# Moving the first projections one row tile ahead, with earlier weights and a quarter of the norms on ScalarE, in a sandwich transformer layer

## What is computed

```python
x = L0_attn_x                                   # (4, 4096, 1024), float32
x = x + layernorm(attn(layernorm(x)))           # 16 heads of 64, causal, ALiBi slopes
x = x + layernorm(ffn(layernorm(x)))            # 1024 -> 4096 -> 1024

# attn
q, k, v = heads(x @ Wq), heads(x @ Wk), heads(x @ Wv)
scores = einsum('bhqd,bhkd->bhqk', q, k) - slopes * dist
attn = softmax(where(causal, -inf, scores) / 8)
return einsum('bhqk,bhkd->bhqd', attn, v) @ Wo + bo
# ffn: x @ w1 + b1, rounded to 1/256, piecewise-linear GELU, @ w2 + b2, rounded
```

## Time and profile before

| | us |
|---|---|
| median of three runs | 1239.48 (1239.38 to 1240.03) |
| the profiled execution's own time | 1238.13 |
| its span, slowest core (6) | 1236.6 |
| spans of the eight cores | 1233.8 to 1236.6 |
| PE, ScalarE, VectorE, GpSimd busy | 1156.5, 984.7, 747.2, 178.7 |

### The profile page before, as it was taken

How to read it: one execution, slowest core, us unless ns; L and a number is a source line. 1 busy time by engine, 2 the same in 40 slices (tenths; PEclk the granted TensorE clock), 3 DMA queues, 4 the chain that set the end, 5 groups by cost and what they waited for, 6 DMA issues and landing times.

```text
span 1236.6 us, 27106 instructions; the slowest of 8 cores (1233.8 to 1236.6 us)
## 1 busy us (share of the span) xinstructions
PE 1156.5 (94%) x11298; PEld 641.0 (52%) x11298; DVE 747.2 (60%) x1607; ACT 984.7 (80%) x1219; POOL 178.7 (14%) x357
## 2 busy tenths in 40 slices
PE   3889989999999999999996999879999999999997
PEld 2566656656566565666654444433444444444443
DVE  7876443332434334343431689996888888888843
ACT  3449999999999999999999478887777777777720
POOL 4520010010100000000010344340111111111110
PEclk9999999999999999999999999999999999999999
DMA  9942543343533312111129664447333333443211
GB/s 260 276 149 55 102 71 58 58 86 61 92 57 70 65 32 52 27 32 27 33 50 171 225 199 155 147 127 161 110 109 112 110 111 112 128 128 111 77 68 69
DMA packets 62870, 128.00 MB, mean 104 GB/s; under 512 B 9238, under 2 KB 26134, under 8 KB 62108
## 3 DMA queue, kind: packets, MB, share of 16 engines
q1 hardware_dynamic: 53900, 101.10, 27.3%
q0 software_dynamic: 8848, 25.17, 13.0%
HBM read 117.84 MB, written 25.17 MB: 116 GB/s over the span
## 4 chain that ended last, share of the span: by engine, by line
PE 74%; DVE 12%; ACT 8%; DMA 3%; POOL 1%; issue 1%; SPq 0%; DVEq 0%; POOLq 0%; ACTq 0%
PE pW L898 18%; PE pF L825 14%; PE pjb L310 12%; PE S L403 9%; PE acc L456 9%; PE pjb L342 8%; ACT P L419 6%; DMA xst<-x_full 2%; DVE x L701 2%; PE pja L310 1%; DVE bst L229 1%; DVE bst L230 1%; DVE g L869 1%; DVE g L863 1%; DMA W<-wqkv 1%
## 5 line engine op out<-in xcount | busy, mean ns | idle before, releaser
L419 ACT ACTIVATE P<-S,biasT 128x1024 bf16<-128x1024 f32 (+1 forms) x576 | 563.0, 1083 | 21.2 <-PE S L403 19.5
L825 PE MATMUL pF<-xl2T,w1s 128*128 128x512 bf16 x1024 | 260.1, 383 | 11.2 <-ACT cu L840 11.2
L898 PE MATMUL pW<-w2s,hq 128*128 128x512 bf16 x1024 | 253.2, 380 | 3.0 <-ACT pW L923 3.0
L456 PEld LDWEIGHTS acc<-V,P 128*128 128x128 bf16 x4352 | 162.6, 97 | 53.0 <-DVE ctx L474 10.9
L403 PE MATMUL S<-Q,K 64*128 64x512 bf16 (+3 forms) x1280 | 174.9, 350 | 14.7 <-ACT P L419 12.8
L456 PE MATMUL acc<-V,P 128*128 128x66 bf16 x4352 | 180.0, 193 | 3.7 <-DVE ctx L474 2.0
L310 PE MATMUL pjb<-xlT,W 128*128 128x512 bf16 x648 | 167.1, 382 | 2.1 <-DVE kst L320 0.8
L825 PEld LDWEIGHTS pF<-xl2T,w1s 128*128 128x128 bf16 x1024 | 100.0, 99 | 132.3 <-ACT cu L840 13.2
L898 PEld LDWEIGHTS pW<-w2s,hq 128*128 128x128 bf16 x1024 | 100.2, 98 | 124.4 <-issue 4.0
L320 DVE CAST kst<-pjb 128x512 bf16<-128x512 f32 x81 | 56.0, 691 | 132.6 <-PE pjb L310 128.8
L840 ACT ACTIVATE cu<-pF,b1s 128x512 int32<-128x512 f32 x128 | 87.7, 685 | 58.7 <-PE pF L825 58.7
(11 more groups left out here) (80 smaller groups left out, 1079.8 us busy)
## 6 DMA issues: line engine op xcount, KB each, us to landing
w1s<-w1bf SPq DMA_DIRECT2D x128, 256.0 KB, 3.1
xst<-x_full SPq DMA_DIRECT2D x32, 512.0 KB, 10.1
K<-kst SPq DMA_DIRECT2D x128, 64.0 KB, 2.0
Q<-kst SPq DMA_DIRECT2D x128, 64.0 KB, 2.3
w1bf<-w POOLq DMA_DIRECT2D x32, 256.0 KB, 3.8
w2s<-w POOLq DMA_DIRECT2D x8, 1024.0 KB, 21.1
x<-x_full SPq DMA_DIRECT2D x16, 512.0 KB, 4.4
x2scr<-x SPq DMA_DIRECT2D x16, 512.0 KB, 3.0
```

The source lines that it names most:

```text
L419: t = put("scalar", lambda io: io.activation(out=P3[:, :, c0:512], in_=S[s][:].rearrange("p (o c) -> p o c", o=2)[:, :, c0:512], func=AF.E ...
L456: io.matmul(acc[:, q * 66:(q + 1) * 66], P[p][:, at:at + 128], zv[:, o, j, hh, :], start=st, stop=sp, skip_group_check=True),
L825: t = put("tensor", lambda io, c=c: io.matmul(pF[b][:], w1s[n % 4][:, c * 128:(c + 1) * 128], xl2T3[g][:, c, :], start=(c == 0), stop=(c = ...
L898: t = put("tensor", lambda io, ft=ft, hf=hf: io.matmul(pO[b][:, hf * 512:(hf + 1) * 512], slot_of(g, ft, tl), w2s[:, ft * 1024 + hf * 512: ...
```

## The change

Three edits. Every fourth tile (t % 4 == 3) is normed by ScalarE as an activation with a scale and a bias; for it `stats2` is asked for `nm`, minus the mean times `rs`, two GpSimd operations more. The weights of head pair 0 are requested in the iteration of tile 0 in place of tile 2; those of head pair 1 stay at tile 10. Pieces are put from the iteration of tile 8 on in place of tile 9, and a block is open one iteration sooner.

```diff
@@ -259,12 +259,17 @@
 
         def ln_a(t, t_x):
             k, tk = stats((xst[t % NX][:, 0:512], xst[t % NX][:, 512:1024]), [t_x])
-            return k, stats2(k, tk)
+            return k, stats2(k, tk, neg=t % 4 == 3)
 
         def ln_b(t, k, t_r):
-            tn = put("vector", lambda io: io.tensor_scalar(
-                out=xl[t % 4][:], in0=xst[t % NX][:], scalar1=mv[k][:, 0:1], scalar2=rs[k][:, 0:1],
-                op0=ALU.subtract, op1=ALU.mult), after=[t_r, xlfree[t % 4]], inc=True)
+            if t % 4 == 3:
+                tn = put("scalar", lambda io: io.activation(
+                    out=xl[t % 4][:], in_=xst[t % NX][:], func=AF.Identity, bias=nm[k][:],
+                    scale=rs[k][:, 0:1]), after=[t_r, xlfree[t % 4]], inc=True)
+            else:
+                tn = put("vector", lambda io: io.tensor_scalar(
+                    out=xl[t % 4][:], in0=xst[t % NX][:], scalar1=mv[k][:, 0:1], scalar2=rs[k][:, 0:1],
+                    op0=ALU.subtract, op1=ALU.mult), after=[t_r, xlfree[t % 4]], inc=True)
             xfree[t % NX] = tn
             slot_free[k] = [tn]
             tm = None
@@ -501,11 +506,11 @@
                 ln_b(*pend)
             if t + NX - 1 < 32:
                 t_load[t + NX - 1] = ln_load(t + NX - 1)
-            if t in (2, 10):
+            if t in (0, 10):
                 t_w[t // 10] = load_w(t // 10)
             pend = (t, k, t_r)
-            if t > 8:
-                pieces(4, (t - 1) // 8)
+            if t > 7:
+                pieces(4, t // 8)
         ln_b(*pend)
         if gen:
             for _ in gen:
```

## The result

The changed kernel takes 1244.37 us (median), the kernel before 1239.48; the ratio is 1.0036, 95% interval 1.0026 to 1.0046. The forecast was 1243.8. Some executions of every kernel here, three of nine of the changed one, are disturbed and some per cent longer, and no ratio uses them. The profiled execution took 1244.25 us with a span of 1242.7, against 1238.13 and 1236.6. That is 6.1 more, as the profiled execution before lies 1.35 under its median and this one at it; the medians differ by 4.9.

The account below looks back on a forecast made before the run. PE was taken to bound the kernel, with attention PE's own length; 0.3 + 2.17 - 1.0 + 4.9 - 0.2 + 0.1 - 2.0 = +4.3 us gave 1243.8 against the median 1239.48, range 1240.0 to 1247.2.

Parts of the forecast that it names:

- The norms on ScalarE: First stage: norms queue behind copy and kst eviction; tiles 15, 19, 27, 31 cost 4.9 us, tile 23 gains 0.2.
- Rival B: First stage: ScalarE's norms find it free, the 4.9 falls away, V intervals shrink; -1.6 us, or 1235 to 1238; chance 0.10.
- The head start: Projections from tile 8: late tile 7 uses up the tile gained; first projection at 29.7 to 30, an estimate.
- The landing: Head pair 1's weights in the first stage: land 0.3 us later, bounds -1.8 and +1.5; PE still waits some 2 us.
- the 44 that the prediction named as a sign of being wrong: First stage: the prediction is wrong if head pair 1's weights land before 44 us.
- Rival A: First stage: norms hurt as forecast, but pair 1's weights land 1.8 us early, no clock drop; +1.5, 1241.0; chance 0.18.
- the terms 0.3 + 2.17 - 1.0: Around pair 1's weights: landing 0.3 us later, one tile interval more behind it 2.17, low clock avoided 1.0.
- the 1.23 of tile 15: First stage, before tile 15's transposes: PE idles 1.23 us for the ScalarE norm, 3.40 against 2.17.
- costed at nothing as cover: First stage, tile 11: its ScalarE norm's delay hides under PE's stall for head pair 1's weights, so zero cost.
- The low clock: PE after the stall for pair 1's weights: a 2 us wait keeps 2.4 GHz; credit 1.0 of 1.67 us.
- the terms of the first stage: Up to the first score: 0.3 + 2.17 - 1.0 + 4.9 - 0.2 + 0.1 us, all terms but attention's.
- Attention: Attention stage, PE's own length: the V unit moved out gains 2.0 us, bounds 1.0 and 2.4.

Follow-up runs that it names:

- e1: Kernel before with only every fourth norm put on ScalarE; weights of head pair 0 at tile 2, pieces from tile 9 as before: ratio 1.0025, +3.1 us.
- e3: Changed kernel with only the ScalarE norm moved ahead in its queue, right behind its own tile's statistics: ratio 1.0001 against the kernel before.
- e2: Kernel before with weights of head pair 0 at tile 0 and pieces from tile 8, all norms on VectorE: ratio 1.0013, +1.6 us.
- e4: Kernel before with only the weights of head pair 0 asked for at tile 0: ratio 0.9985, -1.9 us.
- e8: Kernel before with one V unit moved from attention to the end of the first stage: no ratio on record, profiled execution 1240.82 us.
- e9: e4 with the norms of tiles 22, 23, 24, 29, 30 on ScalarE, put ahead in its queue: ratio 0.9956 against the kernel before, -5.5 us.

## Why the prediction was right, and where it was not

**The norms on ScalarE.** The step that decided. 3.40 us from T(t-1) to T(t) was forecast and 3.34 measured, at the four tiles named, and 2.9 at tile 23 (70.89 to 73.75, 2.86). From T(15) to T(31) core 6 took 42.48 us, 3.23 more than before; three such intervals less tile 23's gain were forecast at 3.5. e1 shows the cost by itself, e3 that it is the place in the queue. Rival B fell with it: even with the norms out of PE's way (e3) the time is that of the kernel before and not under it.

**The head start.** That tile 7 would use it up was right in kind: landing near 24 was forecast, its statistics start at 24.68. It was too small in size, as the first projection came at 31.48 and not near 30; tile 10's statistics are 0.9 late and not 0.3. The forecast's chain left out that the norm of tile 7, too, stands behind a copy: its statistics were complete at 28.23, the copy of tile 6 began at 28.02, and the norm at 28.93. PE was then to come to head pair 1's weights at about 44.5 and to wait 2 us; it came at 45.5 and didn't wait.

**The landing.** This step failed. The weights were to land near 46.6. On core 6 they landed 9.1 us behind the first request at 33.22, at 42.3, where the earlier trace rows has 14.0; on the eight cores at 42.1 to 46.0, against 44.9 to 46.8 before. Six of them are under the 44 that the prediction named as a sign of being wrong. Rival A had the earlier landing right, but not its time (1241.0): PE came too late to use it. Why they land sooner stays open. Tile 16's place in the queue is not enough: e2 has the same order of requests and 43.2 to 49.6, and e4, where tile 16 keeps its place, has them 1.1 sooner as well.

So the terms 0.3 + 2.17 - 1.0 are right in their sum and wrong as a path, and that is luck. No tile interval followed a landing; PE went on at its own pace. On the mean of the cores T(15) came 2.8 us later (50.3 to 53.1), where these terms and the 1.23 of tile 15 make 2.7. It is made up otherwise (an estimate from the rows). The first projection is 0.8 later, one tile interval more lies behind it (2.2), and the norms add 1.2 at tile 15 and 1.1 at tile 11. The stall of 2.3 is gone, and so is the low clock, 0.6 (1.67 on three of eight cores). About 0.4 is left over. Tile 11, costed at nothing as cover, counts in full once there is no stall to hide it.

**The low clock.** As forecast it is gone, but not because PE waited 2 us in place of 3: it did not wait for these weights at all. The credit of 1.0 was for the slowest core. The latest first score is 98.66 (core 5), against 93.28 before (core 4), +5.4, where the terms of the first stage add to +6.3. The mean core has +6.1.

**Attention.** This step failed. The moved V unit was to give 2.0 us, bounds 1.0 and 2.4. Attention is 0.6 shorter in the changed kernel, 0.9 from e4 to e2 and 0.5 in e8; as it is 0.4 shorter in e1 without such a unit, these are no finer than that. The reading of the earlier trace rows was at fault: 3.6 us of waiting for ScalarE in 547 was taken for "PE alone binds". The windows of core 6 before (columns as in the earlier trace rows) show both engines nearly full, PE busy for 98% and ScalarE for 96% of the stretch:

```profile
93.00:640.00 547.00, 537.69 (x7672) 336.78 (x7672) 214.41 (x576) 525.92 (x538) 28.46 (x63) 1.00 0.30 56
```

Work taken from one turned in large part into a wait for the other (PE's 3.6 became 4.6). The total came out within 0.6 by luck as well: this miss (1.4 too much gain) stands against the 0.2 to 0.9 by which the first stage was overstated, and against medians that lie closer together than the profiles.

**The edits apart.** The forecast costed the earlier weights at nothing but the landing's 0.3. By themselves they gain 1.9 us (e4). In its profile PE arrives later at a wait that it had anyway, the weights land a little sooner, and no clock is lost. In the whole change the stall and the low clock go in the same way.

## What to carry to other kernels

An instruction moved to an engine with idle time takes the place in that engine's queue that the program gives it: before pricing its duration, name what stands ahead of it there and whether that in turn waits for the engine you want to relieve. The same 1.24 us norm cost 1.2 us a tile behind such a copy and eviction, 0.3 ahead of them, and gained about 0.7 at tiles where the other engine's queue was the hold-up. A cost that is written off as hidden under a stall comes back when the same change removes the stall, as at tile 11. And where two engines are both over 95% busy, neither's waits alone price a unit of work: measure by moving one unit, as the answer here was a quarter to a half of its duration one way and more than half of it the other.

## What the runs showed of the hardware

The length of PE's wait goes with its clock afterwards, but doesn't decide it alone. Before, cores that idled 1.2 to 2.9 us ahead of head pair 1's projections kept 2.4 GHz. Those that idled 3.04 to 3.56 us ran the next tile at 1.2 GHz, at a cost of 1.7 us on core 6. The windows of core 4 (columns as in the earlier trace rows), which idled 3.56 us:

```profile
46.00:48.00 2.00, 1.31 (x4) 0.58 (x6) 2.00 (x4) 0.00 (x0) 1.23 (x2) 0.62 1.08 253
48.00:50.00 2.00, 2.00 (x12) 1.27 (x11) 1.97 (x5) 0.08 (x1) 1.23 (x2) 0.53 1.01 355
```

In e2 a core that idled 2.97 us kept the clock and those from 3.31 us on lost it. But in e3 core 3 idled 2.14 us and lost it too, again for 1.7 us, while in e8 cores that idled 2.24 and 2.40 us kept it. The window of e3's core 3:

```profile
45.78:50.00 4.22, 4.22 (x18) 2.17 (x19) 4.12 (x10) 1.25 (x2) 2.44 (x6) 0.60 1.05 298
```

Weights asked for 5.4 us earlier did not take their turn evenly from the tiles behind them: in the changed kernel tile 6's statistics began 2.75 us behind tile 5's and tile 7's 5.8 us behind tile 6's, where 3.19 (23.30 to 26.49) was the longest before. The second weights landed 12.0 to 14.1 us behind their request in the three kernels that ask for the first ones at tile 2 (before, e1, e8). In the five that ask at tile 0 and still at tile 10 (the changed one, e2, e3, e4, e9) it was 8.8 to 14.3, on the mean of the cores 9.8 in the changed kernel against 13.3 before. By the Trainium skill ("DMA: Bandwidth & Descriptors", "Queues, rings and completion order") the engines take turns between queues; no run here shows why one tile bore so much of it.
